# Three experts and a convolution on one Trainium2 core: two experts more in half passes, the convolution's tiles set between expert units, one DMA for each channel's read

## The chip, the cores and the metric

One Trainium2 chip; the kernel runs on one of its cores. The metric is the time of one launch in microseconds (us) on the device, lower is better. Engines: PE (TensorE, matmuls), DVE (VectorE), ACT (ScalarE), POOL (GpSimd), and SP (SyncE), which here issues every DMA.

## What is computed

x is (2, 8, 256, 256) in f32: batch b, channel e, rows n, features d. Four residual layers follow one another. Each first normalises x over groups of two channels (`_gn`, G=4: mean and variance for each batch and pair of channels).

```python
def _expert(x, w1, b1, w2, b2):            # layers L0, L2, L3; L3 with the exact gelu
    h = jnp.einsum('bend,edh->benh', x, w1) + b1[None, :, None, :]      # H = 1024
    h = jax.nn.gelu(h)
    return jnp.einsum('benh,ehd->bend', h, w2) + b2[None, :, None, :]

def _conv(x, weight, bias):                # layer L1: 3x3, weights sign(w) * mean|w|
    xp = jnp.pad(x, ((0, 0), (0, 0), (1, 1), (1, 1)), mode='edge')
    return lax.conv_general_dilated(xp, binarize(weight), (1, 1), 'VALID') + bias[None, :, None, None]

x = x + _expert(_gn(x), L0...)
x = x + _conv(_gn(x), L1...)
x = x + _expert(_gn(x), L2...)
x = x + _expert(_gn(x), L3...)
```

So channel e of an expert layer needs only its own weights and the statistics of its pair of channels, but the convolution needs all eight channels of a batch, and the first channel pair behind it needs the convolution of all rows of that batch.

## The kernel before

x lies in SBUF as `XT` (features on partitions, both batches). The 24 experts (E = 0 to 7 of L0, 8 to 15 of L2, 16 to 23 of L3) are worked one after another in **units**: t = 0 to 7 is a block of 128 hidden features. A unit is `g1` (six matmuls into a `G1` bank), gelu on ACT into `HR`, a rounding copy `Hh` on ACT, the rest `Hl = HR - Hh` on DVE (`h_lo`), and `g2` (six matmuls into two `ACC` banks). f32 precision comes from splitting each operand into a high and a low fp32r part, hence three products for each pair. PE runs g1 of unit u and then g2 of unit u-2. After a pass `evict` (DVE, L734) adds ACC to `XT`. The weights of the next expert are split during the units of the one before (`w_hi` on ACT L546, `w_lo` on DVE L699); its input is normalised (`norm`, L709) and split (`x_hi` L553, `x_lo` L714).

A **job** is the statistics of a channel pair: bn_stats (L653), bn_aggr (L660), a matmul that averages over partitions (L995), `deviate` (L667 to L671), a second matmul (L1001), `add_eps` (L677), the power -0.5 on POOL (L493), `scale_shift` (L686, L687). It is spread over the units of the expert before.

An expert is usually one **pass** of 512 columns (both batches). Experts 7, 8 and 9 (`HALVED`) are two passes of 256 columns, one for each batch; 8 and 9 are **crossed**: 8 on batch 0, 9 on batch 0, 8 on batch 1, 9 on batch 1.

The convolution stands between expert 7 and expert 8 as a block of 20 **tiles** (10 for each batch). Its layout `XC` holds 16 rows of 8 channels on 128 partitions, 19 overlapping blocks of rows in a batch. Each channel is written to DRAM (`store_x1`) and read back into XC by four DMAs (`load_xc`, L405 to L412). A tile is: normalise (POOL L499), high part `Ch` (ACT L617), low part `Cl` (DVE L894), six matmuls (PE L1122), scale and bias in PSUM (ACT L622), add into XC (DVE L903). Then SP returns the rows to `XT` with 20 DMAs for each batch (`give_back`, L436). Only when the 20 of batch 0 have landed can job 9, the statistics of channels 0 and 1 of batch 0, begin:

```python
            conv_low(q - 3)
            dve.wait_ge(x2_in[0], 16 * pieces_back())
            sums(9, 0)
            sums_done(9)
            aggregate(9)
            conv_add(q - 5)
```

Of the kernel before, what the change touches and what calls it, by code (L numbers as in the profile page):

```python
# [63 lines left out]
def pieces_back():  # L67

    return sum(len(rows_back(k)) for k in range(NBLK))


HALVED = (C - 1, C, C + 1)
CROSSED = (C, C + 1)


def units(E):

    return 2 * HT if isinstance(E, int) and E in HALVED else HT


def order(P):

    if isinstance(P, int) and 2 * P in CROSSED:
        return [(ee, b * HT + t) for b in range(B) for ee in range(2) for t in range(HT)]
    return [(ee, t) for ee in range(2) for t in range(units(2 * P + ee if isinstance(P, int) else None))]


def slots(E, layer=None):

    return HT * (E + sum(E > h for h in HALVED)) if isinstance(E, int) else (  # L90
        HT * E + (len(HALVED) * HT if layer else 0))


def slot_of(E, t, layer=None):

    if isinstance(E, int) and E in CROSSED:
        return slots(C) + (t // HT * 2 + E - C) * HT + t % HT
    return slots(E, layer) + t


def norm_of(E, b):

    return 2 * C + 2 * b + E - C if isinstance(E, int) and E in CROSSED else 2 * E + b


def evicts(E, layer=None):

    return DC * (E + sum(E > h for h in HALVED)) if isinstance(E, int) else (
        DC * E + (len(HALVED) * DC if layer else 0))


def evicts_for(E, b, layer):


    if not isinstance(E, int):
        return evicts(E - 1, layer)
    if E == C - 1:
        return evicts(E) if b else evicts(E - 1)
    if E in CROSSED:
        return evicts(C) + (2 * b + E - C - 1) * DC if b or E > C else evicts(C)  # L120
    return evicts(E) - DC if E == C + 2 else evicts(E - 1)

ONE_BATCH = {7: 0, 8: 1, 9: 0, 10: 1}


def batches(J):

    return (ONE_BATCH[J],) if isinstance(J, int) and J in ONE_BATCH else tuple(range(B))


def jobs_weighed(J, late):

    return B * J - sum(J > j for j in ONE_BATCH) if isinstance(J, int) else B * J - (len(ONE_BATCH) if late else 0)

USUAL = dict(sums=0, aggregate=1, mean=3, deviate=3, variance=5, eps=6, scale=7)


def jobs_of(P, ee, f):


    if not isinstance(P, int):
        if f == 0:
            return [(2 * P + ee, USUAL, 2 * P - 2 if ee else 2 * P + 2, P - 1 if ee else NPAIR)]  # L150
        return [] if ee else [(P + 7, USUAL, 2 * (P - NPAIR * f) + 2, NPAIR)]
    E = 2 * P + ee
    if E == 0:
        return [(1, dict(sums=4, aggregate=5, mean=7, deviate=7), 2, NPAIR)]
    if E == 1:
        return [(1, dict(variance=0, eps=0, scale=1), 2, NPAIR)]
    if E == 7:
        return [(6, dict(sums=0, aggregate=1, mean=4, deviate=4, variance=6, eps=7, scale=8), 4, 2),
# [1004 lines left out]
```

## Time and profile before

| | |
|---|---|
| median of 3 runs | 614.93 us (614.17 to 615.29) |
| the profiled execution | 614.43 us, of which the span from first to last instruction is 612.4 us |
| TensorE's mean granted clock | 0.989 of 2.4 GHz |
| PE busy | 97% of the span (594.5 us), weight loads 82% |
| ACT, DVE, POOL busy | 70%, 69%, 5% |
| convolution's matmuls | 204.4 to 240.4 us |

A matmul's duration in a row is longer than the distance to the next one, since they are pipelined: the distance between starts is what it costs. "Idle before" is what an engine waited for.

### The profile page before, as it was taken

To read this page: it belongs to the slowest core of one execution; us is meant where nothing else is said; L and a number is where in the kernel's file an instruction comes from. 1 tells how busy PE (TensorE), PEld (TensorE's weight loads), DVE (VectorE), ACT (ScalarE), POOL (GpSimd) and SP (SyncE) were. 2 spreads that over 40 slices of the span, in tenths; PEclk is the share of its full clock that TensorE was granted. 3 is DMA by queue.
4 is the path that set the end of the run, shared out by engine and by line. 5 is a ranking of instruction groups with operands and counts; after the bars stand their busy time and mean duration, and the time that the engine had idled before them with its cause. 6 is when DMAs were issued, how large, how long until landed. Compare 5 with 4: busy or idle time off the path is not lost.

```text
span 612.4 us, 9520 instructions
## 1 busy us (share of the span) xinstructions
PE 594.5 (97%) x2973; PEld 501.0 (82%) x2973; DVE 423.2 (69%) x857; ACT 430.3 (70%) x741; POOL 31.3 (5%) x52
## 2 busy tenths in 40 slices
PE   7999999999999896999999999999999999999997
PEld 7778888888889775999888888888888888888885
DVE  4867968768787796767865866866775675675532
ACT  5766767677777685769867777777767777777743
POOL 2000000000000451000000000000000000000000
PEclk9999999999999997999999999999999999999999
DMA  8673355455363599801332323223234244234001
GB/s 273 188 238 105 113 163 176 119 165 152 108 178 103 197 116 110 177 2 63 109 105 77 130 68 118 88 74 133 70 109 132 86 123 136 86 116 142 17 19 69
DMA packets 56342, 72.80 MB, mean 119 GB/s; under 512 B 4064, under 2 KB 50160, under 8 KB 56304
## 3 DMA queue, kind: packets, MB, share of 16 engines
q1 hardware_dynamic: 56304, 72.33, 41.5%
q8 instruction: 19, 0.31, 0.2%
q14 instruction: 19, 0.16, 0.1%
HBM read 59.70 MB, written 8.42 MB: 111 GB/s over the span
## 4 chain that ended last, share of the span: by engine, by line
PE 87%; DVE 4%; DMA 2%; issue 2%; SPq 2%; POOL 1%; ACT 1%; DVEq 0%; POOLq 0%; ACTq 0%
PE G L1016 42%; PE ACC L1039 14%; PE ACC L1034 14%; PE ACC L1035 14%; DMA W2raw<-in_L_conv_w 1%; DVE Cl L894 1%; DMA XT<-XC 1%; PE TR L1052 1%; SPq L374 1%; DVE XC L903 1%; DVE BN L653 1%; SPq L436 1%; PE ACC L1122 1%; PE TR L982 1%; PE STAT L995 0%
## 5 line engine op out<-in xcount | busy, mean ns | idle before, releaser
L720 DVE TENSOR_TENSOR Hl<-HR,Hh 128x512 fp32r<-128x512 f32 (+1 forms) x216 | 136.2, 631 | 158.8 <-ACT Hh L563 157.5
L559 ACT ACTIVATE HR<-G,BT 128x512 f32<-128x512 f32 (+1 forms) x216 | 138.3, 640 | 137.1 <-PE G L1016 135.9
L1016 PE MATMUL G<-Xh,W1l 128*128 128x512 f32 (+1 forms) x432 | 163.9, 379 | 3.3 <-issue 1.9
L1016 PE MATMUL G<-Xl,W1h 128*128 128x512 f32 (+1 forms) x432 | 158.7, 367 | 0.0
L1016 PE MATMUL G<-Xh,W1h 128*128 128x512 f32 (+1 forms) x432 | 158.5, 367 | 0.0
L1034 PE MATMUL ACC<-Hh,W2l 128*128 128x512 f32 (+1 forms) x432 | 156.5, 367 | 0.0
L1035 PE MATMUL ACC<-Hh,W2h 128*128 128x512 f32 (+1 forms) x432 | 156.2, 366 | 0.0
L563 ACT ACTIVATE Hh<-HR 128x512 fp32r<-128x512 f32 (+1 forms) x216 | 126.3, 585 | 8.7
L1039 PE MATMUL ACC<-Hl,W2h 128*128 128x512 f32 (+1 forms) x432 | 123.5, 367 | 0.6 <-DVE Hl L720 0.6
L1016 PEld LDWEIGHTS G<-Xh,W1l 128*128 128x128 f32 x432 | 82.0, 190 | 16.1 <-issue 2.2
L1016 PEld LDWEIGHTS G<-Xh,W1h 128*128 128x128 f32 x432 | 81.9, 189 | 13.6
L1034 PEld LDWEIGHTS ACC<-Hh,W2l 128*128 128x128 f32 x432 | 81.8, 189 | 13.4
L1035 PEld LDWEIGHTS ACC<-Hh,W2h 128*128 128x128 f32 x432 | 81.8, 189 | 13.2
L1016 PEld LDWEIGHTS G<-Xl,W1h 128*128 128x128 f32 x432 | 82.1, 190 | 11.5
L1039 PEld LDWEIGHTS ACC<-Hl,W2h 128*128 128x128 f32 x432 | 78.2, 189 | 14.5 <-DVE Hl L720 1.3
L699 DVE TENSOR_TENSOR W2l<-W2raw,W2h 128x512 fp32r<-128x512 f32 x96 | 65.6, 686 | 4.2 <-ACT W2h L546 3.6
L699 DVE TENSOR_TENSOR W1l<-W1raw,W1h 128x512 fp32r<-128x512 f32 x96 | 65.5, 686 | 2.7 <-ACT W1h L546 2.5
L546 ACT ACTIVATE W2h<-W2raw 128x512 fp32r<-128x512 f32 x96 | 58.9, 616 | 3.6 <-DMA W2raw<-in_L_conv_w 3.6
L546 ACT ACTIVATE W1h<-W1raw 128x512 fp32r<-128x512 f32 x96 | 58.6, 617 | 2.1 <-DMA W1raw<-in_L_conv_w 2.1
L653 DVE BATCH_NORM_STATS2 BN<-XT 128x6 f32<-128x512 f32 (+1 forms) x60 | 37.3, 680 | 3.2 <-DMA XT<-XC 3.2
L493 POOL TENSOR_TENSOR RS<-VE,half 128x2 f32<-128x2 f32 (+1 forms) x18 | 12.8, 708 | 489.4 <-DVE VE L677 489.4
L714 DVE TENSOR_TENSOR Xl<-XN,Xh 128x512 fp32r<-128x512 f32 x48 | 32.9, 686 | 0.6 <-ACT Xh L553 0.4
(73 smaller groups left out, 357.4 us busy)
## 6 DMA issues: line engine op xcount, KB each, us to landing
W1raw<-in_L_conv_w SPq DMA_DIRECT2D x24, 1024.0 KB, 5.1
W2raw<-in_L_conv_w SPq DMA_DIRECT2D x24, 1024.0 KB, 5.6
x_scratch<-XT SPq DMA_DIRECT2D x16, 256.0 KB
out_x<-OUTT SPq DMA_DIRECT2D x16, 256.0 KB, 2.2
XC<-x_scratch SPq DMA_DIRECT2D x16, 252.0 KB
XT<-XC SPq DMA_DIRECT2D x34, 112.0 KB
NAT<-in_x SPq DMA_DIRECT2D x6, 512.0 KB, 8.4
NAT<-in_x SPq DMA_DIRECT2D x4, 256.0 KB, 3.6
```

What stands on the lines that cost most here:

```text
L493: nc.gpsimd.tensor_tensor(RS[:, bs], VE[:, bs], half[:, bs], ALU.pow).then_inc(rs_done, 1)
L546: nc.scalar.activation(dst, src, ACT.Copy).then_inc(whi, 1)
L559: nc.scalar.activation(HR[:, t % 2, 0:n], G1[t % 2][:, 0:n], func, bias=BT[:, bass.ds(col, 1)]).then_inc(gelu_done, 1)
L563: nc.scalar.activation(Hh[:, t % RING, 0:n], HR[:, t % 2, 0:n], ACT.Copy).then_inc(hhi, 1)
L653: nc.vector.bn_stats(BN[:, b, i], at).then_inc(bn_done, 1)
L699: nc.vector.tensor_tensor(dst, src, high.bitcast(F32), ALU.subtract).then_inc(wlo, 1)
L714: nc.vector.tensor_tensor(Xl[:, par, :, b], XN[:, b], Xh[:, par, :, b].bitcast(F32), ALU.subtract).then_inc(xlo, 1)
L720: nc.vector.tensor_tensor(Hl[:, t % RING, 0:n], HR[:, t % 2, 0:n], Hh[:, t % RING, 0:n].bitcast(F32), ALU.subtract).then_inc(hlo, 1)
L1016: ins = nc.tensor.matmul(G1[t % 2][:, 0:width(b)], w[:, ee, c, col], rhs, start=n == 0, stop=n == len(parts) - 1)
L1034: nc.tensor.matmul(banks[m][:, 0:n], W2l[:, ee, t8, col], high, start=t8 == 0, stop=False)
L1035: nc.tensor.matmul(banks[m][:, 0:n], W2h[:, ee, t8, col], high, start=False, stop=False)
L1039: ins = nc.tensor.matmul(banks[m][:, 0:n], W2h[:, ee, t8, col], Hl[:, t % RING, 0:n], start=False, stop=t8 == HT - 1)
```

## The change

The expert loops, which were partly hardware loops with rules in functions (`order`, `slots`, `jobs_of`, `norms_of`), are written out from tables over one list of passes, `PASSES`, with one running number u for all units. In it:

- experts 6 and 7 are crossed like 8 and 9, so there are now four experts in halves: passes P6 = (6, batch 0), P7 = (7, 0), P8 = (6, 1), P9 = (7, 1), P10 = (8, 0), P11 = (9, 0), P12 = (8, 1), P13 = (9, 1);
- the convolution is no block of its own: the tiles of batch 0 stand between the units from P8's last to P9's fifth, those of batch 1 between P10's fifth and P11's second (`CONV_AT`);
- the statistics of channels 0 and 1 after the convolution are taken as a whole in the last unit of P9 (batch 0) and of P11 (batch 1), behind the evict of that pass;
- a tile uses the `ACC` pair that is free or `TR`; mean|w| is multiplied in the DVE's add and the bias is added to XC by ACT; the edge copies move from DVE to POOL;
- each channel of a batch is read into XC by one DMA with 19 overlapping windows of 16 rows, not by four;
- `HR`/`Hl`, `XN`/`Xl` and `CN`/`Cl` share memory, so the low part is written in place, and HR has four buffers;
- g2 waits for its weights a quarter at a time; the weights of expert 8 are split in P9 and P10, those of expert 9 in P10 and P11.

```diff
+CROSSED = (C - 2, C - 1, C, C + 1)
+PASSES = ([(E, BOTH) for E in range(C - 2)]
+          + [(E, (b,)) for pair in (CROSSED[0:2], CROSSED[2:4]) for b in range(B) for E in pair]
+          + [(E, BOTH) for E in range(C + 2, EXPERTS)])
...
+        if E == C:
+            steps = [unit(P9, t) for t in (4, 5, 6, 7)] + [unit(P10, t) for t in (0, 1, 2, 3)]
+        elif E == C + 1:
+            steps = [unit(P10, t) for t in (4, 5, 6, 7)] + [unit(P11, t) for t in (1, 3, 5, 7)]
...
+CONV_AT = {unit(P8, 7): (0,), unit(P9, 0): (1, 2, 3), unit(P9, 1): (4, 5), unit(P9, 3): (6, 7, 8), unit(P9, 4): (9,),
+           unit(P10, 4): (10,), unit(P10, 5): (11, 12), unit(P10, 6): (13,), unit(P10, 7): (14, 15),
+           unit(P11, 0): (16, 17), unit(P11, 1): (18, 19)}
...
+    (0, (0,), 0.5, dict(sums=unit(P9, 7), aggregate=unit(P9, 7), mean=unit(P9, 7), variance=unit(P9, 7),
+                        eps=unit(P9, 7), scale=unit(P9, 7))),
...
+    (0, (1,), 0.5, dict(sums=unit(P11, 7), aggregate=unit(P11, 7), mean=unit(P11, 7), variance=unit(P11, 7),
+                        eps=unit(P11, 7), scale=unit(P11, 7))),
...
-                    sp.dma_start(XC[written, b, 0:last, 1:N + 1],
-                                 rows[0:OUTR * last].rearrange("(k j) n -> j k n", j=OUTR)).then_inc(done, 16)
-                    sp.dma_start(XC[further, b, 0:last - 1, 1:N + 1],
-                                 rows[OUTR:OUTR * last].rearrange("(k j) n -> j k n", j=OUTR)[0:KS - 1]
-                                 ).then_inc(done, 16)
-                    sp.dma_start(XC[further, b, last - 1, 1:N + 1], rows[OUTR * last:OUTR * last + KS - 1]
-                                 ).then_inc(done, 16)
-                    sp.dma_start(XC[all_rows, b, last, 1:N + 1], rows[LASTROW:DP]).then_inc(done, 16)
+                    first = x1_dram[e, 0:ROWS, b * N:(b + 1) * N]
+                    windows = bass.AP(tensor=first.tensor, offset=first.offset,
+                                      ap=[[TOK, ROWS], [OUTR * TOK, NBLK], [1, N]])
+                    sp.dma_start(XC[e:PART:C, b, :, 1:N + 1], windows).then_inc(done, 16)
...
+                nc.scalar.activation(Ch[:, q % CRING, 0:w], CN[:, q % CRING, 0:w], ACT.Copy
+                                     ).then_inc(chi, 1)
+                at = XC[:, b, own, 1:N + 1]
+                nc.scalar.activation(at, at, ACT.Identity, bias=conv_bias[:, 0:1]).then_inc(cbiased, 1)
...
+                if waits_for_conv and t == 0:
+                    g2(u - 2)
+                    g2(u - 1)
+                    for J in jobs_at("mean", u - 1):
+                        mean_over_partitions(J)
+                        variance_over_partitions(J)
+                g1(u)
+                for q in tiles[0:1]:
+                    conv_tile(q)
+                if u >= 2 and not (waits_for_conv and t < 2):
+                    g2(u - 2)
+                for q in tiles[1:]:
+                    conv_tile(q)
...
+                if u in (unit(P9, 7), unit(P11, 7)):
+                    evict(p)
```

What the change moves, at the three places the prediction speaks of. First PE, at the way from the convolution of batch 0 into expert 8 (STAT is the bank of the two statistics matmuls, BAND the convolution's weights). Before, the block's last two tiles:

```order
L1122 MATMUL ACC_1<-Cl,BAND 128x512 x3
L995 MATMUL STAT<-MV,ones_mean 128x1
L1122 MATMUL ACC_0<-Ch,BAND 128x512 x3
L1122 MATMUL ACC_0<-Cl,BAND 128x512 x3
L1001 MATMUL STAT<-Q,ones_mean 128x1
L1122 MATMUL ACC_1<-Ch,BAND 128x256 x3
L1122 MATMUL ACC_1<-Cl,BAND 128x256 x3
L1016 MATMUL G_0<-Xh,W1l 128x256
```

and now, at the end of P9:

```order
L968 MATMUL ACC_0<-Hh,W2l 128x256
L969 MATMUL ACC_0<-Hh,W2h 128x256
L968 MATMUL ACC_1<-Hh,W2l 128x256
L969 MATMUL ACC_1<-Hh,W2h 128x256
L973 MATMUL ACC_0<-Hl,W2h 128x256
L973 MATMUL ACC_1<-Hl,W2h 128x256
L930 MATMUL STAT<-MV,ones_mean 128x1
L936 MATMUL STAT<-Q,ones_mean 128x1
L951 MATMUL G_0<-Xh,W1l 128x256
```

The two STAT matmuls stood among tiles of batch 1; now they stand between the last g2 of P9 and the first g1 of P10, with nothing else there.

Second DVE, the same job. Before:

```order
L653 BN_STATS BN<-XT 128x6 x2
L660 BN_AGGR MV<-BN 128x2
L903 TENSOR_TENSOR XC<-ACC_1,XC 128x2x256
L894 TENSOR_TENSOR Cl<-CN,Ch 128x516
L667 COPY MEAN<-STAT 128x1
L668 TENSOR_TENSOR DM<-MV,STAT 128x1
L671 SCALAR_TENSOR_TENSOR Q<-DM,MV 128x1
L903 TENSOR_TENSOR XC<-ACC_0,XC 128x2x256
L677 TENSOR_SCALAR VE<-STAT 128x1
```

and now:

```order
L744 SCALAR_TENSOR_TENSOR XT<-ACC_0,BT,XT 128x256
L744 SCALAR_TENSOR_TENSOR XT<-ACC_1,BT,XT 128x256
L665 BN_STATS BN<-XT 128x6 x2
L671 BN_AGGR MV<-BN 128x2
L677 COPY MEAN<-STAT 128x1
L678 TENSOR_TENSOR DM<-MV,STAT 128x1
L681 SCALAR_TENSOR_TENSOR Q<-DM,MV 128x1
L687 TENSOR_SCALAR VE<-STAT 128x1
L694 COPY ST<-RS 128x1
L695 SCALAR_TENSOR_TENSOR ST<-MEAN,RS 128x1
L717 TENSOR_SCALAR XN<-XT,ST 128x2x256
L723 TENSOR_TENSOR Xl<-XN,Xh 128x2x256
```

The job is one unbroken series behind the evict (the first two rows), and the same twelve rows stand once more at the end of P11. Third DVE, in the last units of P11, just ahead of that second series:

```order
L729 TENSOR_TENSOR Hl<-HR,Hh 128x256 x2
L708 TENSOR_TENSOR W2l<-W2raw,W2h 128x512
L729 TENSOR_TENSOR Hl<-HR,Hh 128x256 x2
L708 TENSOR_TENSOR W2l<-W2raw,W2h 128x512
L744 SCALAR_TENSOR_TENSOR XT<-ACC_0,BT,XT 128x256
```

The last quarter of expert 9's second weights is split behind the last Hl of P11, where before the weights of expert 9 were all split before expert 8's fifth unit.

## Rows read from the trace of the kernel before

**Rows 1.** The page: the chain that ended last, by engine, share of the span.
```profile
PE 87%; DVE 4%; DMA 2%; issue 2%; SPq 2%; POOL 1%; ACT 1%; DVEq 0%; POOLq 0%; ACTq 0%
```

**Rows 2.** Timeline of PE: start us, us, what; first matmuls of units two apart.
```profile
165.14 0.39 PE L1016 MATMUL G<-Xh,W1l 128*128 128x512 f32 x1
...
170.58 0.39 PE L1016 MATMUL G<-Xh,W1l 128*128 128x512 f32 x1
...
189.54 0.28 PE L1016 MATMUL G<-Xh,W1l 128*128 128x256 f32 x1
...
192.42 0.28 PE L1016 MATMUL G<-Xh,W1l 128*128 128x256 f32 x1
```

**Rows 3.** Timeline of PE: last g2 before the convolution, first g1 behind.
```profile
202.70 0.40 PE L1039 MATMUL ACC<-Hl,W2h 128*128 128x256 f32 x2
...
242.79 0.36 PE L1016 MATMUL G<-Xh,W1l 128*128 128x256 f32 x1 [1.95 <-issue]
...
248.87 0.28 PE L1016 MATMUL G<-Xh,W1l 128*128 128x256 f32 x1
```

**Rows 4.** Form of L1122's matmuls.
```profile
L1122 PE MATMUL ACC<-Ch,BAND x60: 281/398/774, 204.4 to 239.7; 128*128 128x512 f32 x54, 128*128 128x256 f32 x6
```

**Rows 5.** A stretch of 1 us: PE, PEld, DVE, ACT, POOL busy, PEclk, DMA share, GB/s.
```profile
234.00:235.00 1.00, 0.00 (x0) 0.00 (x0) 0.90 (x2) 0.00 (x0) 0.00 (x0) 0.54 0.93 68
```

**Rows 6.** Timeline of job 9 on all engines, 234 to 243 us.
```profile
234.10 1.29 DVE L653 BATCH_NORM_STATS2 BN<-XT 128x6 f32<-128x512 f32 x2 [3.16 <-DMA XT<-XC]
235.42 0.21 DVE L660 BATCH_NORM_AGGREGATE MV<-BN 128x2 f32<-128x12 f32 x1
...
236.70 0.15 DVE L667 COPY MEAN<-STAT 128x1 f32<-128x1 f32 x1
...
236.95 0.22 DVE L671 SCALAR_TENSOR_TENSOR Q<-DM,MV 128x1 f32<-128x1 f32 x1
...
239.29 0.16 DVE L677 TENSOR_SCALAR VE<-STAT 128x1 f32<-128x1 f32 x1 [1.52 <-PE STAT L1001]
...
240.22 0.15 DVE L686 COPY ST<-RS 128x1 f32<-128x1 f32 x1 [0.43 <-POOL RS L493]
...
240.48 0.55 DVE L709 TENSOR_SCALAR XN<-XT,ST 128x512 f32<-128x512 f32 x1
...
241.35 0.62 ACT L553 ACTIVATE Xh<-XN 128x512 fp32r<-128x512 f32 x1
...
242.00 0.69 DVE L714 TENSOR_TENSOR Xl<-XN,Xh 128x512 fp32r<-128x512 f32 x1 [0.38 <-ACT Xh L553]
```

**Rows 7.** Timeline: the first job's mean matmul and its reader; an evict of a half pass.
```profile
8.40 0.38 PE L995 MATMUL STAT<-MV,ones_mean 128*128 128x2 f32 x2
...
8.82 0.16 DVE L667 COPY MEAN<-STAT 128x2 f32<-128x2 f32 x1 [0.48 <-PE STAT L995]
...
193.20 0.87 DVE L734 SCALAR_TENSOR_TENSOR XT<-ACC,BT,XT 128x256 f32<-128x256 f32 x2
```

**Rows 8.** Timeline of ACT: one unit of a half pass with a weight split.
```profile
185.92 0.47 ACT L559 ACTIVATE HR<-G,BT 128x256 f32<-128x256 f32 x1
...
186.75 0.61 ACT L546 ACTIVATE W2h<-W2raw 128x512 fp32r<-128x512 f32 x1
```

**Rows 9.** Timeline of ACT and SP: a tile's two ACT steps; the last store and next read.
```profile
230.43 0.64 ACT L617 ACTIVATE Ch<-CN 128x516 fp32r<-128x516 f32 x1
230.97 0.73 ACT L622 ACTIVATE ACC<-ACC,conv_bias,conv_mean 128x512 f32<-128x512 f32 x1
...
194.89 0.25 SPq L393 DMA_DIRECT2D x_scratch<-XT  x1
196.50 0.89 SPq L405 DMA_DIRECT2D XC<-x_scratch  x1
```

**Rows 10.** The rows' return: its issues, and DMA share and GB/s while it fills the queues.
```profile
L436 SPq DMA_DIRECT2D XT<-XC x40: 675/801/890, 211.6 to 245.0; - x40
...
216.00:234.00 18.00, 15.44 (x66) 10.87 (x64) 14.27 (x26) 14.31 (x24) 9.61 (x13) 1.00 0.99 115
```

More of the change, by code:

```diff
@@ new lines, in first_pass, with last_pass, unit, halved @@
+def first_pass(E):
+    return pass_of(E, 0)
+def last_pass(E):
+    return pass_of(E, B - 1)
+def unit(p, t):
+    return HT * p + t
+def halved(p):
+    return len(PASSES[p][1]) == 1
+def width(p):
+    return N * len(PASSES[p][1])
+SPLITS = [(p, b) for p, (E, bs) in enumerate(PASSES) for b in bs]
+def split_no(p, b):
+    return SPLITS.index((p, b))
+def evicted_by(p):
+    return DC * (p + 1)
+P6, P7, P8, P9, P10, P11, P12, P13 = (pass_of(E, b) for pair in (CROSSED[0:2], CROSSED[2:4])
+                                      for b in range(B) for E in pair)
@@ new lines, in split_steps, with weight_steps @@
+def split_steps():
+    at = {}
+    for p, b in SPLITS[2:]:
+        if p in (P6, P7):
+            at[unit(p - 1, 2)] = (p, b)
+        elif p == P8:
+            at[unit(P6, 5)] = (p, b)
+        elif p == P9:
+            at[unit(P7, 5)] = (p, b)
+        elif p == P11:
+            at[unit(P10, 4)] = (p, b)
+        elif p == P13:
+            at[unit(P12, 4)] = (p, b)
+        elif p not in (P10, P12):
+            at[unit(p - 1, 2 + 2 * b)] = (p, b)
+    return at
+def weight_steps():
+    at = {}
+    for E in range(1, EXPERTS):
+        p = first_pass(E) - 1
+        steps = [unit(p, t) for t in range(HT)]
+        if E == C:
+            steps = [unit(P9, t) for t in (4, 5, 6, 7)] + [unit(P10, t) for t in (0, 1, 2, 3)]
+        elif E == C + 1:
+            steps = [unit(P10, t) for t in (4, 5, 6, 7)] + [unit(P11, t) for t in (1, 3, 5, 7)]
+        for k, u in enumerate(steps):
+            at.setdefault(u, []).append((E, k))
+    return at
@@ new lines, with jobs_at, job_of, weighed @@
+NJOBS = len(JOBS)
+CONV_JOBS = {b: [J for J, (e, bs, of, _) in enumerate(JOBS) if of == 0 and b in bs] for b in range(B)}
+LAST_CONV_JOB = {b: max(CONV_JOBS[b]) for b in range(B)}
+def jobs_at(stage, u):
+    return [J for J, job in enumerate(JOBS) if job[3].get(stage) == u]
+def job_of(E, b):
+    f, e = divmod(E, C)
+    of = (-1, 0.5, 1)[f]
+    return next(J for J, job in enumerate(JOBS) if job[2] == of and job[0] == e - e % 2 and b in job[1])
+def weighed(J):
+    return sum(len(job[1]) for job in JOBS[:J])
@@ L54, in rows_back @@
 def rows_back(k):
     d, end = OUTR * k, min(OUTR * (k + 1), D)
-    j = d - LASTROW + 1 if k == NBLK - 1 else 1
+    j = 1
     parts = []
@@ L64, in rows_back @@
     return parts
[L67 to L91, printed above, removed]
@@ L94, in slot_of @@
[L94 to L121, printed above, removed]
@@ L126 @@
[L126 to L158, printed above, removed]
-                (7, dict(sums=10, aggregate=11, mean=12, deviate=12, variance=13, eps=13, scale=14), 6, 3)]
-    if E == C:
-        return [(11, dict(mean=9, deviate=9, variance=11, eps=11, scale=12), 2, NPAIR)]
-    if E == C + 1:
-        return [(10, dict(sums=0, aggregate=0, mean=2, deviate=2, variance=3, eps=4, scale=4), 0, NPAIR),
-                (11, dict(sums=5, more_sums=6, aggregate=7), 2, NPAIR)]
-    if P >= 5 and ee == 0 and P + 1 < LAYERS * NPAIR:
-        return [(P + 7, USUAL, (2 * P + 2) % C, NPAIR)]
-    return []
```

901 lines of the change are left out of this document (411 added, 490 removed).

## The prediction

> **What bounds the kernel now.** I read the page's chain first: 87% of it is PE [rows 1], so time is won only where PE waits or does work that isn't needed. Then PE's timeline. In the long middle two units of 512 columns start 5.44 us apart, so a unit costs 2.72 us and a matmul 0.227; two units of 256 columns start 2.88 us apart, 1.44 a unit and 0.120 a matmul [rows 2]. There PE has no holes. Third, the place where it has some: the last matmul of g2 of expert 7 has started at 202.82 (two of them in the row from 202.70) and its 0.12 end at 202.94; expert 8's first g1 starts at 242.79 [rows 3]. Between lie 39.85 us. The convolution's own matmuls are 108 of 512 columns and 12 of 256 (the row has those with Ch, half of them [rows 4]), 24.5 + 1.4 = 25.9 us. So 13.9 us of the block are waits and slow clock. Behind it, from 242.79 to 248.87, stand 36 matmuls that take 6.08 us where 4.32 are due [rows 3]: another 1.8. The granted clock fell to 1.2 GHz in the wait for the rows' return (0.54 of 2.4 GHz between 234 and 235 us, PE idle [rows 5]). In all **15.7 us** are to be had here, and nowhere else that the change touches.
>
> **What it removes.** The block. If every tile falls between units that have work, the 15.7 us go. I take them off in full and charge below what the new order waits for.
>
> **What it adds, on PE.** One more expert in halves: 16 units of 1.44 for 8 of 2.72, 23.04 - 21.76 = **+1.3 us** [rows 2]. Loops written out: PE ran at the same 2.72 in both kinds of code, so nothing.
>
> **The two borders.** This is the term that decides. At the end of P9 PE does its last two g2 and then, before the first g1 of expert 8, only the two statistics matmuls; DVE first evicts P9, which waits for that last g2, and then does the whole job in one series. Nothing is left to fill PE: P9 is done, P10 needs the result. Counted link by link: the last matmul drains (0.16, its row's 0.28 less the step of 0.12), evict 0.87 [rows 7], two bn_stats 1.29 and the aggregate 0.21 [rows 6], mean matmul until its reader starts 0.42 [rows 7], MEAN to the end of Q 0.47 [rows 6], variance matmul 0.42 like the mean, VE to ST over POOL's power 0.93, ST to XN 0.26, XN 0.55, Xh 0.62, Xl 0.69 [rows 6]. That is 6.9, and with some 0.3 for the handovers between engines **7.2 us** of idle PE. Before, the same series took from 234.10 to 242.69 with tiles among it. Now there are two such borders, at P10 and at P12 (the same twelve instructions): **+14.4 us**. The statistics of batch 1 were spread over expert 9's units before and cost PE nothing; their cover is what is lost at P12.
>
> **The clock behind a border.** 7 us of idle is longer than the idle that made the clock fall in the rows (3.16 us of DVE's wait [rows 6], the clock low at once behind it [rows 5]). The nearest price is the 1.8 us of the stretch behind 242.79. It is a low bound, since part of the slow time was already spent in the last tiles; I take 2.0 each, **+4.0 us**, with 1.7 and 3.5 as the ends.
>
> **Expert 9's last weights.** The second g2 from P11's end (its seventh unit) waits for the fourth quarter of the second weights, which ACT splits behind the gelu of P11's last unit. After that g1 ends: gelu and copy 0.83, the split 0.61 [rows 8], DVE's low part 0.69 (the length of a 512-element subtraction, as Xl [rows 6]), 2.2 with handovers; PE has one g2, 0.72, to do until then. **+1.5 us**, at P12 alone. At P10 the same kind of wait (first quarter of expert 8's) is hidden by g1s at the slow clock; without that it would cost 0.8.
>
> **Pace inside the tiles.** ACT, not PE, is short in P10 and P11. A tile is Ch (0.54 from start to start [rows 9]) plus the bias, now an SBUF pass I put at 0.6 (between 0.54 and the 0.73 of the PSUM one [rows 9]). From P10's fourth unit to P11's first stand ten tiles' steps, six gelu pairs of 0.83, five splits of 0.61 and one Xh of 0.62: 11.4 + 5.0 + 3.1 + 0.6 = 20.1 us. PE's own work there is 6 units and 8 tiles, 8.6 + 10.9 = 19.5. With that little room an ACT that runs its steps in a fixed order is late for one tile's low part (DVE stands in h_lo in front of it) and for expert 9's first weights: **+2.0 us**, from 0.6 (the plain difference) to 4. In batch 0 the same count comes out even, +0.4 for the g2 of P9 that waits for the sixth tile's add.
>
> **The one read for four.** It takes three issues, none longer than the 0.89 us of the first [rows 9], from SP's queue for each channel. It is off the path for seven channels. For the last channel of batch 0 it shortens: evict of P7, 0.9; store, three issues put at 1.0, and its landing, 1.36 from the end of the last (195.14) to the read's issue; that issue 0.89 [rows 7, 9]; then landing, edges, normalise and Ch, about 5, beside 5 units and a g1, 7.9 us, from evict to tile 0. So +0.7 (0 to 2.5). Four reads would make it later by three issues, under 2.7.
>
> **Sum.** -15.7 + 1.3 + 14.4 + 4.0 + 1.5 + 2.0 + 0.4 + 0.7 = +8.6. On the profiled execution's 614.43 us that is 623.0; the median of the runs shown is 0.5 above it, so 623.5, 1.4% slower.
>
> **Rivals.**
> *The rows come back too late (slower still).* P10's series begins when evict ends and the 20 return DMAs of batch 0 have landed. DMA moves them at 115 GB/s with all queues full [rows 10], 0.97 us for 112 KB. Counting from P9's first g1, PE is through with P9 at 24.6 us and bn_stats could start at 25.7. Tile 6 is added at about 14.5; seven returns are left, 6.8 us, with 0.8 of issue [rows 10] and 1.4 of landing, 23.5. So 2 us of room; it decides from there. The 40 returns took 33.4 us to issue [rows 10], 0.84 each, so SP isn't short. If DVE's adds slip by more, each us late is a us of time: 625 to 629.
> The Trainium skill, "DMA: Bandwidth & Descriptors", section "Why a DMA increments its semaphore by 16 and not by 1", says that a DMA is split over the largest number of engines up to 16 that divides the slowest dimension on both sides. By it the pieces of 2, 4 and 12 rows last as long as a whole one, and the room shrinks by under 1 us; no row here shows one piece's engines.
>
> *The borders cost far less (faster).* The series is short enough, or the clock does not fall, so that the block's 15.7 us outweigh it. Were each border 4 us at full clock and ACT never late: 614.4 - 15.7 + 1.3 + 8.0 + 1.5 = 609.5, 610 for the median. It decides where both borders with their clock cost under 10 instead of my 18.4. For it: PE's and DVE's times above come from a stage where tiles stood between. Against: I counted the lengths of the instructions, not their waits, and each needs the one before.
>
> *Only the inner waits vanish (slower, but less).* Borders as counted, but clock at 1.7 and ACT and DMA fully hidden: -15.7 + 1.3 + 14.4 + 3.4 = +3.4, to 618.5.
>
> *No difference.* The terms on both sides cancel: this needs borders of about 5 us each with the rest as counted.
>
> **How the numbers follow.** My forecast (+5 to +12) 0.58, slower still 0.16, slower but less 0.12, no difference 0.04, faster 0.10. A measurement here can tell about 0.2%, 1.2 us, from no change. Range: from 617.0, which leaves out the faster and equal cases (0.14), to 629.0, the end of the late rows, above which I leave under 0.06; the open prices (pace 0.6 to 4, clock 3.4 to 7, first tile 0 to 2.5) add up to 619.6 to 630.3 at their ends, which will not all come together.
>
> **What would show it.** In the profile after: two stretches of PE idle of about 7 us, ahead of the first g1 of P10 and P12, with evict, bn_stats and the rest of the job on DVE in them, ended by `Xl`; the clock at half behind each. The convolution's matmuls spread over two groups of about 20 us each, and g1's start-to-start between tiles near 0.72 plus 1.36 a tile. If bn_stats of the first border waits for `XT<-XC`, the rows are late. A g2 waiting for `W2l` ahead of the second border is the 1.5. Wrong I would be if PE stays busy over the borders, or if tiles wait on Ch or Cl by much more than 3 us in all.

## The result, and the profile after

The changed kernel takes **646.43 us** (645.71 to 647.82), the kernel before, run beside it, 614.74; the ratio is 1.0518, 95% interval 1.0498 to 1.0539. Forecast were 623.5 and slower: the direction was right, the size was not (+31.7 us, forecast +8.6), and the result lies above the stated range. The profiled execution took 646.52 us, its span is 644.7.

The page: busy time, the granted clock in 40 slices, and the chain by engine.

```profile
PE 607.6 (94%) x3069; PEld 512.7 (80%) x3069; DVE 427.2 (66%) x869; ACT 430.7 (67%) x757; POOL 33.5 (5%) x56
...
PEclk8999999999999967897999999999999999999999
...
PE 80%; ACT 4%; issue 4%; DVE 4%; DMA 3%; SPq 2%; POOL 1%; DVEq 0%; ACTq 0%; POOLq 0%
```

PE had 87% of the chain before [rows 1] and has 80% now, but is also busy 13 us longer. So there are new waits, and the same matmuls have become slower (the 96 more of the expert in halves are 1.3 us of the 13). The waits first. What PE waited for between 190 and 296 us (sum in us, times, longest):

```profile
PE STAT L930 <- DVE MV L671: 7.2, 3, 2.4
PE G L951 <- issue: 6.3, 2, 3.2
PE ACC L968 <- DVE W2l L708: 3.5, 3, 1.6
PE ACC L987 <- DVE Cl L793: 3.2, 2, 3.1
PE ACC L987 <- issue: 2.2, 1, 2.2
PE ACC L987 <- ACT Ch L590: 2.0, 1, 2.0
PE G L951 <- DVE W1l L708: 2.0, 1, 2.0
PE STAT L936 <- DVE Q L681: 1.1, 2, 0.6
PE ACC L968 <- DVE XC L802: 0.6, 1, 0.6
```

And where these stand, in PE's timeline: the end of P9, the series of the first border, P10, batch 1's first tile, expert 9's last W1 quarter, the last of its W2 quarters, the first g1 of P12.

```profile
222.13 0.40 PE L973 MATMUL ACC<-Hl,W2h 128*128 128x256 f32 x2
...
225.88 0.38 PE L936 MATMUL STAT<-Q,ones_mean 128*128 128x1 f32 x2 [0.57 <-DVE Q L681]
229.42 0.55 PE L951 MATMUL G<-Xh,W1l 128*128 128x256 f32 x1 [3.16 <-issue]
...
234.74 0.59 PE L930 MATMUL STAT<-MV,ones_mean 128*128 128x1 f32 x2 [2.42 <-DVE MV L671]
...
242.51 0.99 PE L987 MATMUL ACC<-Ch,BAND 128*128 128x512 f32 x3 [2.04 <-ACT Ch L590]
246.57 1.65 PE L987 MATMUL ACC<-Cl,BAND 128*128 128x512 f32 x3 [3.07 <-DVE Cl L793]
...
263.79 0.36 PE L951 MATMUL G<-Xh,W1l 128*128 128x256 f32 x1 [1.99 <-DVE W1l L708]
...
286.09 0.36 PE L968 MATMUL ACC<-Hh,W2l 128*128 128x256 f32 x1 [1.64 <-DVE W2l L708]
...
294.64 0.55 PE L951 MATMUL G<-Xh,W1l 128*128 128x256 f32 x1 [3.15 <-issue]
```

The last g2's matmul starts at 222.25 (the second of the first row), its 0.12 end at 222.37, and the first g1 of expert 8 starts at 229.42: 7.05 us, against 7.2 forecast. The second border is 7.05 (287.59 to 294.64). DVE's timeline in the first border shows the series that was counted link by link, from the evict to the low part:

```profile
222.56 0.88 DVE L744 SCALAR_TENSOR_TENSOR XT<-ACC,BT,XT 128x256 f32<-128x256 f32 x2
223.36 1.27 DVE L665 BATCH_NORM_STATS2 BN<-XT 128x6 f32<-128x512 f32 x2
224.67 0.21 DVE L671 BATCH_NORM_AGGREGATE MV<-BN 128x2 f32<-128x12 f32 x1
225.35 0.16 DVE L677 COPY MEAN<-STAT 128x1 f32<-128x1 f32 x1 [0.47 <-PE STAT L930]
...
226.30 0.16 DVE L687 TENSOR_SCALAR VE<-STAT 128x1 f32<-128x1 f32 x1 [0.47 <-PE STAT L936]
...
227.39 0.55 DVE L717 TENSOR_SCALAR XN<-XT,ST 128x512 f32<-128x512 f32 x1
228.63 0.69 DVE L723 TENSOR_TENSOR Xl<-XN,Xh 128x512 fp32r<-128x512 f32 x1 [0.70 <-ACT Xh L567]
```

Behind both borders PE runs at the lower of its two rates. These are windows of 229.4 to 234 and 294.6 to 299 us (PE, PEld, DVE, ACT, POOL busy, then the granted clock, DMA share, GB/s). In [rows 5] the granted clock was as low (0.54), there with PE idle.

```profile
229.40:234.00 4.60, 2.90 (x12) 2.63 (x12) 1.87 (x4) 2.71 (x6) 0.00 (x0) 0.50 0.28 68
...
294.60:299.00 4.40, 4.36 (x20) 4.39 (x21) 1.75 (x4) 1.93 (x5) 0.00 (x0) 0.50 0.01 4
```

The account compares the time of a stretch with what its matmuls take at their full rate [rows 2]; the difference is called excess here. From the first g1 of P6 to that of expert 10 there are 40.7 us of excess, where before there were 15.4, plus 1.3 for the fourth halved expert: 26.7 of the 32.1 us between the two profiled runs. Of the rest, 1.2 is a later first g1 of all (a scatter between executions, as shown below), and 4.2 lie between expert 10 and the end, where the change alters no order. The 40.7 are:

- tile 0 of batch 0: 2.3;
- the two borders: 7.05 each;
- behind the first border, from 229.42 to 239.59: 5.6, a wait of 2.4 for job 9's statistics and 3.2 of half clock;
- batch 1's first tile: 6.3, and 1.7 of slow clock behind it;
- expert 9's last W1 quarter: 2.0, and 1.8 of slow clock behind it;
- three waits for `W2l`, with their handovers: 4.0;
- the slow clock behind the second border: 2.2;
- 0.7 in small pieces.

### The profile page after: what moved, and what is told of

The parts are those of the page before. It is cut to its first block, busy times and chain, and to the rows that moved or that the text cites. A ratio compares the mean times of both kernels' runs of the same rounds, so it can differ in the third digit from the quotient of the medians.

```text
span 644.7 us, 8733 instructions
## 1 busy us (share of the span) xinstructions
PE 607.6 (94%) x3069; PEld 512.7 (80%) x3069; DVE 427.2 (66%) x869; ACT 430.7 (67%) x757; POOL 33.5 (5%) x56
## 4 chain that ended last, share of the span: by engine, by line
PE 80%; ACT 4%; issue 4%; DVE 4%; DMA 3%; SPq 2%; POOL 1%; DVEq 0%; ACTq 0%; POOLq 0%
PE G L951 37%; PE ACC L968 13%; PE ACC L973 13%; PE ACC L969 12%; PE ACC L987 2%; DMA W1raw<-in_L_conv_w 1%; DMA W2raw<-in_L_conv_w 1%; DVE BN L665 1%; ACT HR L577 1%; PE TR L1000 1%; SPq L401 1%; ACT W2h L562 1%; ACT XC L593 1%; ACT W1h L562 1%; PE TR L987 1%
## 5 line engine op out<-in xcount | busy, mean ns | idle before, releaser
L951 PE MATMUL G<-Xh,W1l 128*128 128x512 f32 (+1 forms) x448 | 168.2, 375 | 8.3 <-issue 6.3
L968 PE MATMUL ACC<-Hh,W2l 128*128 128x512 f32 (+1 forms) x448 | 161.4, 366 | 4.1 <-DVE W2l L708 3.5
L951 PE MATMUL G<-Xh,W1h 128*128 128x512 f32 (+1 forms) x448 | 163.3, 365 | 0.0
L951 PE MATMUL G<-Xl,W1h 128*128 128x512 f32 (+1 forms) x448 | 163.1, 364 | 0.0
L951 PEld LDWEIGHTS G<-Xh,W1l 128*128 128x128 f32 x448 | 86.3, 193 | 21.4 <-issue 8.8
L951 PEld LDWEIGHTS G<-Xh,W1h 128*128 128x128 f32 x448 | 86.2, 192 | 13.3
L951 PEld LDWEIGHTS G<-Xl,W1h 128*128 128x128 f32 x448 | 86.5, 193 | 12.1
L969 PEld LDWEIGHTS ACC<-Hh,W2h 128*128 128x128 f32 x448 | 85.4, 191 | 13.2
L567 ACT ACTIVATE Xh<-XN 128x512 fp32r<-128x512 f32 x48 | 29.6, 619 | 18.0 <-DVE XN L717 17.9
L665 DVE BATCH_NORM_STATS2 BN<-XT 128x6 f32<-128x512 f32 x60 | 37.3, 679 | 0.0
```

The costliest lines, as they stand in the source:

```text
L567: nc.scalar.activation(Xh[:, par, :, b], XN[:, par, :, b], ACT.Copy).then_inc(xhi, 1)
L665: nc.vector.bn_stats(BN[:, J % 2, b, i], XT[:, :, b, e + i]).then_inc(bn_done, 1)
L951: ins = nc.tensor.matmul(G1[u % 2][:, 0:n], w[:, par, c, col], rhs, start=i == 0, stop=i == len(parts) - 1)
L968: nc.tensor.matmul(acc(p, m), W2l[:, par, t, col], high, start=t == 0, stop=False)
L969: nc.tensor.matmul(acc(p, m), W2h[:, par, t, col], high, start=False, stop=False)
```

## The experiments

Each was timed beside the kernel before, whose medians were 614.0 to 615.5. In the expected texts a theory A and a theory B are rivals, each with the time that it would give.

Besides the median of whole executions there is a finer measure: the time, in the profiled execution, from the first g1 of expert 8 to that of expert 10, called **the middle** here. It is 89.19 us in the changed kernel and 88.6 to 89.4 in the four kernels below that leave the order there alone. What lies ahead of it scatters more. The first g1 of all comes anywhere from 15.97 to 18.06 us in the changed kernel and its variants. And the wait at tile 0 (2.36 us in the changed kernel) is followed by 3.4 us at half clock in 11 of these 15 traces, but not in the changed kernel's own; where it is, tile 0 and the units behind it take 1.1 to 1.6 us more.

### Where the buffers lie

Full units take 2.765 us instead of 2.72, in all three layers. The change lays several buffers out anew, `HR` and `Hl` in one place among them; HR/Hl now start at byte 210944 and Hh at 219136 of the partition, both multiples of 2048, where HR, Hh and Hl were at 206464, 210560 and 218752.

```diff
+        sb("shift", [PART, 32])
         with ExitStack() as use:
             HR = sb("HR", [PART, RING, TOK], F32, use)
```

> The changed kernel with nothing but 128 unused bytes per partition ahead of the ring HR, so that HR, Hl and Hh (and what is laid behind them) start 128 bytes further on. In the changed kernel a unit of 512 columns lasts 2.765 us all through both layers, against 2.72 before, though neither its matmuls nor its sizes changed. Theory A (place): the buffers stand elsewhere in SBUF than before (Hh at 219136 instead of 210560), and PE reads them at another pace from there. A shift changes the pitch of the 160 full units, back to about 2.72 if the old place modulo some power of two was the good one: 639 to 645 us. Theory B (order): the loops that are written out, and the wait for the low part that every second g2 now has, cost PE the 0.045 a unit. Then the shift does nothing: 646.4 within 1.2.

641.96 us, ratio 1.0444 (1.0409 to 1.0479). Timeline of PE, the first g1s of units two apart, in the changed kernel and with the shift:

```profile
337.10 0.39 PE L951 MATMUL G<-Xh,W1l 128*128 128x512 f32 x1
...
342.62 0.39 PE L951 MATMUL G<-Xh,W1l 128*128 128x512 f32 x1
```

```profile
336.81 0.39 PE L952 MATMUL G<-Xh,W1l 128*128 128x512 f32 x1
...
342.25 0.39 PE L952 MATMUL G<-Xh,W1l 128*128 128x512 f32 x1
```

5.52 us for two units against 5.44: exactly the old pace, theory A. From expert 10's first g1 to the end, 112 full units, the kernel takes 321.5 us instead of 326.1, so 4.6 us less. The 48 full units ahead of P6 give 0.8. The median gains 4.5 in all: in the trace, the slow clock behind tile 0, which this execution has, takes 1.3 of it back. The counterpart is the kernel before, moved by 384 bytes to such multiples.

```diff
+        sb("shift", [PART, 96])
         HR = sb("HR", [PART, 2, TOK])
```

> The kernel before with nothing but 384 unused bytes ahead of HR, so that HR, Hh and Hl start at 206848, 210944 and 219136, all multiples of 2048 as HR, Hl and Hh do in the changed kernel. Theory A (the place alone makes the slower pace, whatever the order of the code): a full unit goes from 2.72 to about 2.765 us, and 168 full units make 7 us: 620 to 622.5. Theory B (place and the changed kernel's order must come together): 614.7 within 1.2.

```profile
335.10 0.39 PE L1017 MATMUL G<-Xh,W1l 128*128 128x512 f32 x1
...
340.63 0.39 PE L1017 MATMUL G<-Xh,W1l 128*128 128x512 f32 x1
```

619.07 us, ratio 1.0079 (1.0053 to 1.0104): its pitch goes to 5.53 for two units and it loses 5.1 us (7 expected for 168 full units), 3.9 of them behind expert 10's first g1. The place alone does it. Two runs ask which place.

> The changed kernel with the same 128 unused bytes as the first run, but laid between Hl and Hh, so that only Hh starts at 219264 and HR with Hl stays at 210944, a multiple of 2048. The first run brought the unit of 512 columns from 2.765 back to 2.72 us with all three shifted. Theory A (what PE reads: Hh's own place decides, alone or with what engines write beside it at the same offset): all of it again, 641.5 to 643 and a pitch of g2 of 1.36. Theory B (what ACT and DVE write: HR and Hl decide): pitch 1.39 as in the changed kernel, 646.4. Theory C (each of the two has a share): g1 and g2 come apart, one at 1.36 and one near 1.38.

644.37 us (1.0482, 1.0456 to 1.0508). With only Hh off the multiple, six matmuls of g2 take 1.37 instead of 1.39, and those of g1 stay at 1.38. That is theory C: each buffer has its share, and g1 slows although it reads none of the three.

> The changed kernel with 1024 unused bytes ahead of HR in place of 128: HR, Hl and Hh at odd multiples of 1024. Theory A (the fast pace needs only that the buffers are off the multiples of 2048): 2.72 a unit, 642. Theory B (a multiple of 1024 is as bad as one of 2048, since each buffer's slots are 2048 bytes): 2.765, 646.4. A pitch between them if the share is a gradual one.

647.84 us (two executions; 1.0550, 1.0520 to 1.0581), g2 1.39, g1 1.38: a shift by 1024 bytes brings nothing back, theory B.

### The one read for four

Undone in the changed kernel (the four reads of the diff, and its waits):

> The changed kernel with the four reads per channel of the kernel before in place of the one (their source rows and counts as before, so the same bytes). Theory A (off the path): at tile 0 of batch 0 the copy of XC's edges had waited only 0.79 us for the read and DVE's statistics of job 7 ended at the same time, 192.4; three more issues put the read of channel 7 some 1 to 2.7 us later at that place alone. 646.4 to 648.5 us, all of it in the wait of tile 0. Theory B (the one read is the slow one: its 25 packets at an instruction sit on few engines and delay what shares the queues): faster than the changed kernel by over 1.2 us, under 645.

648.27 us, ratio 1.0538 (1.0501 to 1.0575), whose interval overlaps with the changed kernel's. In the trace POOL's edge copy waits 1.79 us for the read instead of 0.79, and PE waits 3.3 us for tile 0 instead of 2.36, so 1.0 more: theory A. (Expert 8 begins 2.4 us later there; the rest is a later start and the slow clock behind tile 0.) Alone, in the kernel before:

```diff
-                    rows = x1_dram[e, :, b * N:(b + 1) * N]
-                    sp.dma_start(XC[written, b, 0:last, 1:N + 1],
...
+                    windows = bass.AP(tensor=first.tensor, offset=first.offset,
+                                      ap=[[TOK, ROWS], [OUTR * TOK, NBLK], [1, N]])
+                    sp.dma_start(XC[e:PART:C, b, :, 1:N + 1], windows).then_inc(done, 16)
```

> The kernel before with the one read per channel alone, and the bottom row stored eleven more times that this read needs; passes, tiles and loops as before. Theory A: the reads lie under the matmuls of both layers for seven channels, and at the block the statistics of batch 0 and the edges decide: 614.7 within 1.5 us, rather earlier than later. Theory B: part of the 31.7 us comes from the one read (an uneven load on the engines, a later landing): over 617 us.

609.93 us, ratio **0.9922** (0.9893 to 0.9950): a little faster than both kernels, which neither theory expected. SP's and DVE's timeline (with `SPq`, the queue):

```profile
209.65 0.56 SPq L404 DMA_DIRECT2D XC<-x_scratch  x1
210.26 30.40 SPq L428 DMA_DIRECT2D XT<-XC  x36
...
231.46 1.27 DVE L645 BATCH_NORM_STATS2 BN<-XT 128x6 f32<-128x512 f32 x2
```

The last read's issue took 0.56 us; the four took 2.8 (208.80 to 211.64). The returns behind them on SP's queue began 1.4 us sooner, though PE's work came 0.6 later in this execution, and DVE's `bn_stats`, which had waited 3.16 us for them [rows 6], starts without a wait. The first g1 behind the convolution comes 4.3 us earlier, nearly all of the gain. The rows were there at least 2.6 us sooner (231.46 against 234.10); 1.4 of that is the issue, the rest was not resolved. So about a third of the block's 13.9 us of waits and slow clock hung on how the last rows were read.

### The second border

```diff
-    (0, (1,), 0.5, dict(sums=unit(P11, 7), aggregate=unit(P11, 7), mean=unit(P11, 7), variance=unit(P11, 7),
-                        eps=unit(P11, 7), scale=unit(P11, 7))),
+    (0, (1,), 0.5, dict(sums=unit(P11, 4), aggregate=unit(P11, 4), mean=unit(P11, 5), variance=unit(P11, 6),
+                        eps=unit(P11, 6), scale=unit(P11, 6))),
```

(and P12 treated as an ordinary pass)

> The changed kernel with expert 10's first job (the statistics of its batch 1) spread over the units 4 to 7 of P11, where DVE and ACT have room, instead of standing whole in the border behind P11; P12 becomes an ordinary pass whose input is ready when P11 ends. The changed kernel's second border is 7.05 us of idle PE (287.59 to 294.64) and about 2.2 us of matmuls at half clock behind it. Theory A (the border is the price of the order of the statistics, not of the interleaving): both go, 646.4 - 9.2 = 637 us, between 636 and 639. Theory B (they only move: the job in P11 delays the splits of expert 9's last weights and the low parts, and what PE waits for instead takes most of it back): 642 or more. The clock alone (the idle goes but the rate stays low behind the waits for W2l): 639.5.

638.97 us, ratio 1.0392 (1.0358 to 1.0426): 7.5 less, a little short of theory A's 9.2. The middle takes 81.02 us, 8.2 less.

```profile
283.25 0.36 PE L965 MATMUL ACC<-Hh,W2l 128*128 128x256 f32 x1 [0.71 <-DVE W2l L708]
...
288.04 0.36 PE L948 MATMUL G<-Xh,W1l 128*128 128x256 f32 x1 [2.20 <-issue]
```

Of the border 2.20 us are left ahead of P12 (its `Xl` ends at 287.94, behind `Hl` and `W2l` of the last unit), and the clock still falls behind them.

### Expert 9's second weights

```diff
-            steps = [unit(P10, t) for t in (4, 5, 6, 7)] + [unit(P11, t) for t in (1, 3, 5, 7)]
+            steps = [unit(P10, t) for t in (4, 5, 6, 7)] + [unit(P11, t) for t in (1, 2, 3, 5)]
```

> The changed kernel with one list of numbers changed: expert 9's second weights are split at the units 1, 2, 3, 5 of P11 instead of 1, 3, 5, 7. In the changed kernel PE waits for the low parts of these quarters three times, 0.94, 0.93 and 1.64 us, and a half-split ahead of it brings one more short one. Theory A (each quarter comes one step too late in ACT's fixed order): the waits go, 646.4 - 3.5 to 4.0 = 642.4 to 642.9 us. Theory B (ACT is full in P11, so a split that comes earlier pushes the gelu or the tile behind it, and the wait changes its name): under 1.5 us of gain, 645 or more.

642.98 us (1.0460, 1.0432 to 1.0488). No wait for `W2l` is left: theory A, 3.4 us, and 3.8 in the middle (85.35).

### Batch 1's first tile

```diff
                 h_lo(u)
+                if FIRST_TILES.get(u) == TILES:
+                    conv_low(TILES)
...
-                if u in FIRST_TILES:
-                    conv_low(FIRST_TILES[u])
+                if FIRST_TILES.get(u) == 0:
+                    conv_low(0)
```

> The changed kernel with the low part Cl of batch 1's first tile placed directly behind the unit's Hl on DVE, ahead of the split of expert 8's last second weights and of P11's normalise. In the changed kernel PE waits 2.04 us for Ch of this tile and then 3.07 us for its Cl, and runs 1.7 us slow behind it; DVE stood 3.61 us waiting for W2h with the Cl behind it. Theory A (DVE's order): the 3.07 go and part of the slow clock, 642 to 643.4 us. Theory B (ACT is what is late: Ch comes at the same time, and W2h, which now comes behind, makes g2 wait): the gain is under 1 us.

642.75 us (1.0460, 1.0441 to 1.0478), theory A, 3.7 us. The middle gains 5.5 (83.64): besides the wait for Cl the slow clock behind this tile is gone, and the wait for W1's last quarter is 1.4 instead of 2.0. ACT's and DVE's rows: Cl follows Ch at once, and the split that stood ahead of it now comes behind, where nobody waits for it.

```profile
244.02 0.63 ACT L590 ACTIVATE Ch<-CN 128x516 fp32r<-128x516 f32 x1 [1.14 <-POOL CN L524]
244.68 0.70 DVE L793 TENSOR_TENSOR Cl<-CN,Ch 128x516 fp32r<-128x516 f32 x1 [1.35 <-ACT Ch L590]
...
246.96 0.88 DVE L708 TENSOR_TENSOR W2l<-W2raw,W2h 128x512 fp32r<-128x512 f32 x1 [1.57 <-ACT W2h L562]
```

### Job 9's statistics

```diff
                     norm(P10, 0)
                     x_lo(P10, 0)
+                    sums(9)
+                    aggregate(9)
```

> The changed kernel with bn_stats and aggregate of job 9 (batch 1, channels 6 and 7) moved into the end of the first border, behind Xl of P10, where DVE idles 2.7 us, instead of behind the Hl of P10's first unit. In the changed kernel PE waits 2.42 us for DVE's MV at 234.74, with only two g1 in front, and the same chain ends 9.5 us later in the wait for Ch. Theory A: 2.4 us go at the mean matmul, and the chain eps, scale, constants, Ch ends 1.5 to 2 us sooner, which takes most of the wait of 2.04 for Ch, but the wait for Cl behind W2h stays: 643 to 644.2. Theory B (g1 and g2 at half clock fill the time instead; the chain is decided by ACT's steps): 645.5 to 646.4.

644.48 us (1.0487, 1.0468 to 1.0506), 1.9 us; the middle gains 3.2 (85.99). What PE waits for from 222 to 250 us:

```profile
PE ACC L991 <- DVE Cl L793: 3.1, 1, 3.1
PE STAT L934 <- DVE MV L671: 2.4, 1, 2.4
PE ACC L991 <- ACT Ch L590: 2.1, 1, 2.1
```

The second wait for MV is gone, those for Ch and Cl are as long as they were. Theory A was right on the 2.4 us, and wrong that the chain to Ch would gain on PE: both came earlier by the same.

### All repairs at once, and one step more

> The changed kernel with the four repairs and the shift at once: 128 unused bytes, expert 10's job spread over P11, expert 9's weights one step earlier, Cl of batch 1's first tile ahead, and job 9's sums in the border. Alone they gave 4.5, 7.5, 3.4, 3.7 and 1.9 us. If they are independent terms: 646.4 - 21.0 = 625.4. Where they share the slow clock behind one wait, less: I expect 625 to 628. Under 625 a repair frees another's wait; over 630 ACT's or DVE's whole load in P10 and P11 is the bound, and the single gains were time passed on.

624.83 us (1.0161, 1.0137 to 1.0184): 21.6 less than the changed kernel. The medians' single gains add up to 21.0, which looks like independent terms, but the traces show otherwise. In the middle the four repairs gain 8.2 + 3.8 + 5.5 + 3.2 = 20.7 one by one and 16.1 together (73.12). So the repairs overlap by 4.6 us, 2.6 of them in the last four units of P11 and the border behind: the spread job alone had already shortened the waits for `W2l` from 3.5 to 1.6. One more:

```diff
+                if u == unit(P9, 7):
+                    sums(8)
+                    aggregate(8)
                 for weight in WEIGHTS_AT.get(u, ()):
                     w_lo(*weight)
                 if u == unit(P9, 7):
                     evict(p)
```

> The same as the run before it with one more move: bn_stats and aggregate of job 8 (batch 0 of expert 8) ahead of the last split and of the evict of P9, so that evict runs while PE takes the mean. In the changed kernel the first border is 7.05 us, a series of fourteen steps with the evict (0.88, the mean's reader 1.99 behind the evict's end) in it. Theory A (the border is the plain sum of its series): shorter by 1.1 to 1.3 us than in the run before it, with the sums started at about the time at which the rows are back. Theory B (the rows are not back yet when DVE asks for them, since the last of the 20 returns is issued 3.6 us before P9's last matmul ends): no gain, and DVE waits for XT<-XC.

623.48 us (1.0144, 1.0117 to 1.0171), 1.4 less by the medians, with intervals that overlap; the middle takes 72.53. DVE's rows:

```profile
221.46 1.28 DVE L666 BATCH_NORM_STATS2 BN<-XT 128x6 f32<-128x512 f32 x2
...
223.46 0.87 DVE L745 SCALAR_TENSOR_TENSOR XT<-ACC,BT,XT 128x256 f32<-128x256 f32 x2
```

`bn_stats` starts before the evict and waits for no row, so theory B is out: the return was in time. The border is 6.38 us instead of 7.06, 0.7 shorter and not 1.1 to 1.3: evict and split now stand between MV and MEAN. These kernels are still slower than the kernel before. From the first g1 of P6 to that of expert 10 this one takes 146.9 us, where the changed kernel takes 162.9, so that some 25 of the 40.7 us of excess remain.

### The price of the slow clock

Matmuls that nobody reads keep PE busy in the borders:

```diff
+                        stay_busy(18)
                         mean_over_partitions(J)
+                        stay_busy(6)
                         variance_over_partitions(J)
+                        stay_busy(26)
```

> The changed kernel with matmuls that nobody reads (128x128 of the identity) in the two borders, where PE idles: 18 behind the last g2, 6 behind the mean, 26 behind the variance, about 6.3 us of work at the full clock in 7.05 us. The result is the same. The borders themselves stay 7.05 us long, since each step of their series still needs the one before. Theory A (PE's idle makes the clock fall): the granted clock stays at 1.0 behind both borders; the 2.2 us behind the second go, and behind the first, where 4.6 us of matmuls took 10.2, what is not the wait for the statistics (2.4) goes too, less what then waits for job 9's chain: 646.4 - 3 to 6 = 640.5 to 643.5. Theory B (the clock falls for another reason, or 7 us of such small matmuls don't hold it): 646.4 within 1.5, or slower if they delay the mean.

> The kernel of the twelfth run (four repairs, the shift, the sums first; 623.5 us) with such matmuls in the one border that is left, 7 behind the last g2, 11 behind the mean and 24 behind the variance. Theory A (idle makes the clock fall): in that run the clock stood at 0.71 in the border and 0.72 in the 5.5 us behind it, which cost the 1.28 and 0.95 where 0.72 is due; 1.5 to 2.5 us go: 621 to 622. Theory B (the wait for Ch of batch 1's first tile, 1.75 us there, is set by ACT and POOL and only grows by what PE saves): 623.5 within 1.2, with the clock at 1.0 all the same.

653.13 us (1.0633, 1.0608 to 1.0658) and 627.84 us (1.0207, 1.0178 to 1.0235): I had sized the matmuls at half their length, so that they delayed the mean, the variance and the first g1 (borders of 11.5 us in the first of the two). Both were repeated with about half as many.

> As the thirteenth run, with half of the matmuls that nobody reads: 9 behind the last g2, 3 behind the mean, 14 behind the variance. In the thirteenth run one of them took 0.232 us (50 in 11.8 us), twice what I had reckoned, so that they ran on after DVE's results were there and made each border 4.5 us longer; the granted clock stood at 1.00 in the borders and behind them until PE waited 2.98 us for DVE's statistics of job 9, and 2.0 us of the second border came back behind it. Now they end about when DVE is ready: borders of 7.0 to 7.5. Theory A (idle makes the clock fall): behind the second border 2.0 us go, behind the first 1 to 3: 641.5 to 644. Theory B (the clock saved behind the first border turns into longer waits for job 9's chain): only the 2.0 of the second, 644 to 645.5.

> The kernel of the twelfth run (623.5 us) with 3, 6 and 14 such matmuls in its first border. Theory A: the border keeps its 6.4 us, the clock stays up behind it, and the units that took 1.28 and 0.95 take 0.72 again: 621.5 to 622.5. Theory B (the wait for Ch of batch 1's first tile grows by what is saved): 623.5 within 1.2.

645.41 us (1.0505, 1.0469 to 1.0541) and 623.64 us (1.0141, 1.0107 to 1.0176): theory B both times. From the first of them (borders of 7.06 and 7.05 us again), windows of the second border and behind it, and what PE waits for behind the first and behind the second:

```profile
288.00:293.80 5.80, 5.40 (x47) 5.18 (x46) 3.36 (x11) 0.63 (x1) 0.54 (x1) 1.00 0.34 120
293.80:298.00 4.20, 4.20 (x36) 4.09 (x34) 2.18 (x5) 2.62 (x7) 0.00 (x0) 1.00 0.00 0
```

```profile
235.45 0.59 PE L930 MATMUL STAT<-MV,ones_mean 128*128 128x1 f32 x2 [2.98 <-DVE MV L671]
...
299.29 0.51 PE L973 MATMUL ACC<-Hl,W2h 128*128 128x256 f32 x2 [1.03 <-DVE Hl L729]
```

The clock stays at 1.00 in and behind the borders (0.50 behind them without these matmuls), so PE's idleness did lower it. Behind the second border 2.0 us are saved at first, then 1.3 of them are given back in a wait for `Hl`, which did not exist while PE was slow. Behind the first the wait for MV grows from 2.42 to 2.98. In the trace 0.65 us are left of the saving at the first border and 0.74 at the second. So the slow clock behind both borders cost about 1 us net, less than the intervals can tell. That behind the tiles was not tested.

## Why the prediction was right or wrong

The terms of the sum beside what the accounts of the two profiled executions give, in us:

| term | forecast | measured |
|---|---|---|
| the block's waits and slow clock | -15.7 | -15.4 |
| one more expert in halves | +1.3 | +1.3 |
| the two borders | +14.4 | +14.1 |
| the clock behind them | +4.0 | +5.4 (3.2 and 2.2) |
| expert 9's last second weights | +1.5 | +4.0 |
| pace inside the tiles | +2.0 | +14.2 |
| the g2 that waits for an add, small pieces | +0.4 | +0.7 |
| first tile | +0.7 | +2.3 |
| pace of full units from expert 10 on | none | +4.2 |
| ahead of P6 | none | +1.4 |
| sum | +8.6 | +32.2 |

**Right.** The block's waits go, and two borders come: 7.05 us each against 7.2, by the same links. The series of dependent lengths plus 0.3 for handovers is a good way to price such a place. What counts of the second border with its clock is 7.5 by experiment, 8.2 in the middle (9.2 forecast, of which 2.2 us of idle stayed). The rows come back in time. The read alone changes little in the changed kernel (four reads: "under 2.7" later, measured 1.0 at tile 0). The first four terms alone make the kernel slower, but they come to 5.4 of the 32.2 us.

**The step that failed** is the pricing of everything between the borders from sums per engine, as if each wait could only occur once and only where ACT's sum exceeds PE's; and the buffers' places were put at nothing. By its terms:

- *Pace inside the tiles, +2.0.* I compared sums over ten tiles (20.1 against 19.5). The waits stand at single places in fixed orders, and come to 14.2 us. Batch 1's first tile (6.3, and 1.7 of slow clock) had its Cl on DVE behind a split that ACT did late: 3.7 by experiment, 5.5 in the middle. The statistics of channels 6 and 7 (2.4) I never walked through: only two g1 are in front of their mean, 1.9 by experiment, 3.2 in the middle. W1's last quarter (2.0, with 1.8 of slow clock) is read from the trace alone, as is the wait for Ch of that tile (2.0), which fell to 0.6 when its Cl was moved.
- *"Loops written out: PE ran at the same 2.72 in both kinds of code, so nothing."* The loops are indeed innocent, but the new layout of memory moved the buffers: 4.2 us from expert 10 on, which the shift gives back in full (4.6). The prediction spoke of the layout nowhere. This is shown by the shift and by its counterpart in the kernel before.
- *Expert 9's last weights, +1.5, at P12 alone.* The same lateness occurs at three quarters: 3.4 by experiment.
- *The clock behind a border, 2.0 each.* The clock does fall, at four places in this trace, not two (also behind batch 1's first tile and behind W1's last quarter); behind the borders it costs little net, about 1 us for both, because a slow PE hides the waits that a fast one meets.
- *First tile, +0.7.* 2.3 in the trace. POOL waits 0.79 us for the read, its edge copies end at 192.41, and the constants from job 7 are ready at 192.36: the two come at the same time, so the trace doesn't single one out.

The 1.4 ahead of P6 is mostly the later first g1, and that is within the scatter between executions. What is shown by experiment is the 4.2 of the pace and, in the middle, 16.1 for the four repairs together. The other waits are located in the trace, not removed. The first border wasn't removed by an experiment either; that it costs its 7 us is argued from its length. The two repaired kernels stay 10.8 and 9.5 us above the kernel before, with one border of 7.06 and 6.38 us left in them.

The rival "the borders cost far less" fell with 7 us each. The range's lower sum was also added wrongly: the open prices at their low ends give 620.8, not 619.6, which changes nothing here. And of the 15.7 us that the change was to win, 4.3 were to be had with the single read, for eleven more stored rows of each channel and batch.

## What to carry to other kernels

Before a stage is spread over others to hide its waits, ask what its waits wait for: here a third of them went with three DMA issues fewer ahead of others in one queue. When work is interleaved in fixed orders, walk each series (statistics, weights, low parts) through the new order one by one, since sums per engine see none of the waits; and ask of every edit that changes memory where the buffers come to lie, then compare the pitch of stages that the change doesn't touch. Before single gains are added up, measure them over a stretch between two fixed instructions: the medians here, with the scatter of the parts ahead in them, did not show an overlap of 4.6 us.
